# Causal self attention of a decoder layer: float32r halves kept in SBUF, heads paired in the array, query halves as the unit of order

## What is computed

```python
x = x + _L0_attn_ref(_layernorm(x, axis=-1), L0_attn_Wqkv, L0_attn_bqkv, L0_attn_Wout, L0_attn_bout)
# N_HEADS = 16, HEAD_DIM = 16
qkv = jnp.einsum('bsd,hde->bhse', x, Wqkv) + bqkv[None, :, None, :]
q, k, v = jnp.split(qkv, 3, axis=-1)
score = jnp.einsum('bhsd,bhtd->bhst', q, k)
score = jnp.where(causal[None, None], score, -jnp.inf)
attn = jax.nn.softmax(score / jnp.sqrt(jnp.asarray(HEAD_DIM, x.dtype)), axis=-1)
y = jnp.einsum('bhst,bhtd->bhsd', attn, v)
out = jnp.transpose(y, (0, 2, 1, 3)).reshape(b, s, d) @ Wout + bout
```

## Time and profile before

| what | us |
|---|---|
| median of 3 runs (1902.81 to 1908.55) | 1905.12 |
| the profiled execution's own time | 1912.87 |
| span of the profiled execution | 1911.2 |
| first score matmul starts, in the profile | 111.85 |
| first exponential starts | 156.14 |
| output projection's first transfer | 455.73 |

### The profile page before, as it was taken

One profiled execution on the slowest core, in us unless ns is written; L12 is line 12 of the kernel. 1 busy time (PEld: TensorE's weight loads), 2 busy tenths in 40 slices (PEclk: granted clock), 3 DMA queues, 4 the chain that ended last, 5 costly groups with the idle time before them and its releaser, 6 DMA issues. The chain is left out here.

```text
span 1911.2 us, 28538 instructions
## 1 busy us (share of the span) xinstructions
PE 1438.0 (75%) x10307; PEld 1073.4 (56%) x10307; DVE 1089.6 (57%) x2450; ACT 898.0 (47%) x2137; POOL 308.2 (16%) x338
## 2 busy tenths in 40 slices
PE   4758889988589999789981453588868059999964
PEld 2413333334379999656760231477755059999953
DVE  3657766741655555455668647456553047777753
ACT  1503555553256666331104775366542057887731
POOL 1200000002223333200001525100010600000034
PEclk8858999998799999979995665799887579999987
DMA  2371322200200000110000000211112256766623
GB/s 68 132 99 20 49 35 35 35 2 9 81 1 2 1 1 2 34 39 1 0 23 9 1 6 14 64 35 34 34 47 88 88 188 219 222 216 217 227 85 103
DMA packets 92688, 122.59 MB, mean 64 GB/s; under 512 B 22221, under 2 KB 74051, under 8 KB 92291
## 3 DMA queue, kind: packets, MB, share of 16 engines
q1 hardware_dynamic: 86675, 105.85, 20.5%
q0 software_dynamic: 4912, 14.42, 2.1%
q10 hardware_dynamic: 960, 0.47, 0.1%
HBM read 88.60 MB, written 24.67 MB: 59 GB/s over the span
## 5 line engine op out<-in xcount | busy, mean ns | idle before, releaser
L759 DVE TENSOR_REDUCE sa_top<-ps 128x1 f32<-128x512 f32 (+3 forms) x384 | 197.2, 553 | 96.3 <-PE ps L751 65.3
L787 ACT ACTIVATE sa_probs<-ps 128x1024 f32<-128x1024 f32 (+4 forms) x192 | 150.8, 811 | 204.1 <-PE ps L772 145.6
L751 PE MATMUL ps<-sa_k,sa_q 96*128 96x512 bf16 (+3 forms) x384 | 125.5, 365 | 55.5 <-DMA sa_k<-scr_k 28.5
L1983 PE MATMUL ps<-me_h,me_w_parts 128*128 128x256 f32 x1104 | 142.0, 289 | 14.5 <-DVE me_w_parts L2058 7.9
L1983 PEld LDWEIGHTS ps<-me_h,me_w_parts 128*128 128x128 f32 x1104 | 136.8, 192 | 18.7 <-issue 15.3
L1997 PE MATMUL ps<-me_w_parts,me_mid 128*128 128x256 f32 x1104 | 136.2, 283 | 6.1 <-DVE me_result L2075 6.1
L1997 PEld LDWEIGHTS ps<-me_w_parts,me_mid 128*128 128x128 f32 x1104 | 132.3, 188 | 10.5 <-issue 10.5
L2735 ACT ACTIVATE cx_p<-ps,cx_top 128x154 f32<-128x154 f32 x256 | 97.2, 389 | 86.4 <-DVE cx_top L2799 86.4
L751 PEld LDWEIGHTS ps<-sa_k,sa_q 96*128 96x128 bf16 x384 | 35.1, 98 | 160.7 <-DVE sa_top L759 89.1
L2058 DVE TENSOR_TENSOR me_w_parts<-me_chunk,me_w_parts 128x1024 fp32r<-128x1024 f32 x92 | 112.8, 1226 | 21.4 <-ACT me_w_parts L2023 18.6
L2045 ACT ACTIVATE me_full<-ps,me_b 128x256 f32<-128x256 f32 x184 | 95.0, 517 | 57.6 <-PE ps L1983 54.5
(11 more groups left out here) (397 smaller groups left out, 3530.7 us busy)
## 6 DMA issues: line engine op xcount, KB each, us to landing
me_chunk<-in_L_ffn_W_dram SPq DMA_DIRECT2D x92, 512.0 KB, 5.4
sa_q<-scr_q SPq DMA_DIRECT2D x48, 128.0 KB, 4.8
sa_k<-scr_k SPq DMA_DIRECT2D x48, 128.0 KB, 7.7
moe_rows<-mp_zeros SPq DMA_DIRECT2D x2, 2944.0 KB, 12.7
me_row<-moe_rows SPq DMA_DIRECT2D x23, 256.0 KB, 3.8
moe_results<-me_result POOLq DMA_DIRECT2D x23, 256.0 KB, 3.2
cn_qd<-cn_qh SPq DMA_DIRECT2D x64, 64.0 KB, 2.0
scr_q<-h_part SPq DMA_DIRECT2D x6, 512.0 KB, 3.9
```

The source lines that it names most:

```text
L751: last = pe.matmul(c.ps[:, bank, 0:w], self.q_st[0:96, slot, h, P * sb:P * sb + P], self.k_st[0:96, slot, h, k0:k0 + w], start=True, stop= ...
L759: return dve.tensor_reduce(self.top2[:, k0 // 512, ST * h + sb:ST * h + sb + 1], self.c.ps[:, bank, 0:w], AX.X, ALU.max)
L787: return act.activation(dst, src, ACT.Exp, scale=self.width ** -0.5)
L1983: last = pe.matmul(ps[:, MID + n % 4, 0:RT], w[:, u % 2, 0, i, DM * k + P * b:DM * k + P * b + P], h[:, u % 2, j, k, :], start=(m == 0), s ...
```

## The change

All of setup, context and projection becomes one stage, `front`, and `Attention` with its subclass becomes one class.

- `front` works by quarters of the tokens. x comes in four transfers, each with its own semaphore; the normalisation moves from DVE to ACT; normalised x and the weights are split into a high and a low half in float32r (ACT writes the high half, DVE the difference; POOL both for the weights). Each product is three float32r matmuls (high high, low high, high low) instead of one float32 matmul. Q and K come out as high (ACT) and low half (DVE) and stay in SBUF (`qk_high`, `qk_low`). The bias goes through DRAM once and comes back by five transfers. V gets 17 columns a head instead of 32.
- Staging copies from SBUF to SBUF: three stacks of 16 rows (high, low, high against high, high, low) for each of four heads of a unit, Q by SP, K by POOL, twelve transfers of 64 KB on each. The heads a = 0 and a = 1 of a pair lie at partitions 0 to 47 and 64 to 111, so a score matmul has 48 rows (50 with the two rows of the maximum), and each piece or chunk is now two matmuls, one for each head of the pair, into two banks.
- The grain is half a unit: 512 queries, 16 of them (`SUBS`). The pieces of one half run ahead of its chunks by one half. Exponentials have three buffers, a unit's half and key block each. The banks of pieces, turns and turns back form one ring of three. The count of reductions, masks, exponentials and weigh matmuls, and their widths, summed over a unit, stay as they are.
- The order of PE, DVE and ACT comes from `order()`, which lays out planned times for DVE and ACT with fixed costs and sorts.

The core of the diff:

```diff
+                for j, (i, m) in enumerate(blocks):
+                        terms = [(k, a, b) for k in range(KD) for a, b in ((wh, xh), (wh, xl), (wl, xh))]
+                        for n, (k, a, b) in enumerate(terms):
+                            last = pe.matmul(ps[:, bank, :], a[:, i, k, P * m:P * m + P], b[:, k, 512 * g:512 * g + 512],
+                                             start=(n == 0), stop=(n == len(terms) - 1))
...
+    def order(self):
+        items, dve, act = [], 0.0, 0.0
+        for k in range(len(SUBS)):
+            for n, (p, sb, k0, w) in enumerate(self.pieces(k)):
+                items.append((dve, "piece", k, n))
+                dve += 2 * (0.075 + w / 960)
+            items.append((dve, "join", k, 0))
+            items.append((dve + 1.2, "turn", k, 0))
+            dve += 1.0
+            act = max(act, dve + 5.0)
+            for n, (kb, p) in enumerate(self.chunks(k)):
+                items.append((act - 0.9, "chunk", k, n))
+                act += 0.12 + 2 * self.span(k, kb)[1] / 1200
+                if p == 1:
+                    items.append((act + 0.9, "weigh", k, kb))
+            items.append((act + 1.0, "copy", k, 0))
+            items.append((act + 3.0, "out", k, 0))
...
+                for a in range(2):
+                    pool.memset(self.k[64 * a + 32:64 * a + 64, :, :, :].bitcast(F32), 1.0).then_inc(s["made"].sem, 1)
+                pool.wait_ge(s["made"].sem, s["made"].at(2))
...
+                def take(m):
+                    if m >= self.MAX_RING:
+                        pe.wait_ge(s["freed"].sem, s["freed"].at(m - self.MAX_RING + 1))
+                    return m % self.MAX_RING
...
+                    banks = [take(m) for m in uses["piece", k, n]]
+                    for a in range(2):
+                        r = slice(64 * a, 64 * a + 3 * DH)
+                        last = pe.matmul(ps[:, banks[a], 0:w], self.q[r, slot, half, p, q0:q0 + P], self.k[r, slot, p, k0:k0 + w],
+                                         start=True, stop=not diagonal)
+                    if diagonal:
+                        for a in range(2):
+                            pe.matmul(ps[:, banks[a], w - P:w], c.identb[:, :], c.maxmask[:, :], start=False,
+                                      stop=True).then_inc(s["filled"].sem, 1)
...
-                last = pe.matmul(out[:, 0:qw], self.k_st[0:KROWS, slot, h, P * kb:P * kb + P],
-                                 self.q_st[0:KROWS, slot, h, P * kb + q0:P * kb + q0 + qw],
-                                 start=True, stop=q0 > 0)
```

More of the change, by code:

```diff
@@ L108, in new_stage @@
         self.signals = {}
[L111 to L152, removed]
 class LayerNorm:
@@ L230, in done, with front @@
             self.s[k].passed(n)
[L233 to L242, removed]
+VC = DH + 1
+def front(c, ct, hi, lo, v_all, scratch):
     nc, ps = c.nc, c.ps
     wqkv, bqkv = c.arg["L0_attn_Wqkv"], c.arg["L0_attn_bqkv"]
+    scr_b = scratch("scr_b0", [3, H, DH], F32)
+    G = NT // 4
@@ L246, in project_self @@
     with ExitStack() as ctx:
[L247 to L260, removed]
+        sb = lambda n, shape, dt=F32: c.sb(ctx, "fr_" + n, shape, dt)
+        raw_ctx = sb("ctx", [MH, 4, DC])
+        w = sb("w", [P, KD, H, 3 * DH])
+        wh, wl = sb("wh", [P, 3, KD, D], F32R), sb("wl", [P, 3, KD, D], F32R)
+        bias, bias_v = sb("b", [P, 2, KD]), sb("bv", [P, H, DH])
+        stats, mv = sb("stats", [P, NT, 6]), sb("mv", [P, NT, 2])
@@ L266, in _ @@
+                sp.dma_start(raw_ctx[:, :, :], c.arg["ctx_768"].rearrange("b (i m) d -> m (b i) d", m=MH)).then_inc(c_in.sem, 16)
+                sp.wait_ge(b_out.sem, b_out.at(16))
                 for i in range(2):
[L267 to L278, removed]
+                    for m in range(KD):
+                        sp.dma_start(bias[:, i, m:m + 1],
+                                     scr_b[i, 8 * m:8 * m + 8, :].rearrange("h (e a) -> (h e) a", a=1)).then_inc(b_in.sem, 16)
@@ L292, in _ @@
             @block.tensor
             def _(pe):
[L294 to L309, removed]
@@ L815, in _ @@
+                pe.wait_ge(const.sem, const.at(2))
+                turn(0)
                 pe.wait_ge(c_in.sem, c_in.at(16))
@@ new lines, in self_layer @@
+def self_layer(c, ct, scratch):
+    with ExitStack() as c0:
+        o_tok = c.sb(c0, "o_tok0", [P, NT, D], F32)
+        with ExitStack() as c1:
+            v_all = c.sb(c1, "v_all0", [P, NT, H, VC], F32)
+            hi, lo = c.sb(c1, "qk_high", [P, 2 * KD, N], F32R), c.sb(c1, "qk_low", [P, 2 * KD, N], F32R)
+            front(c, ct, hi, lo, v_all, scratch)
+            c.new_stage()
+            SelfAttention(c, c1, v_all, hi, lo, o_tok).run()
+        c.new_stage()
+        project_out(c, "po0", o_tok, KD, c.arg["L0_attn_Wout"], c.arg["L0_attn_bout"])
```

839 lines of the change are left out of this document (408 added, 431 removed).

## The result

| | us |
|---|---|
| before, median of 4 runs | 1904.49 |
| after, median of 4 runs (1951.86 to 1983.10) | 1971.08 |
| ratio after to before, 95% interval | 1.031 (1.024 to 1.039) |
| the profiled execution after: own time, span | 1968.88, 1966.8 |
| predicted | 1833 (1788 to 1880) |

A forecast was written before the change was run, and what follows sets the result against it. No engine is full; the loop from exponential to weigh step sets attention's pace. First score 83 + half speed 4 + eight units 276 + tail 20 = 383 us instead of 455.2; 1905 - 72 = 1833 us, range 1788 to 1880.

The forecast's parts named there:

- Front: Start to end of projection: first projection matmul at 16 us, end at 59 us instead of 84.1.
- Staging: Between front and attention: POOL's fill 10.5 us, twelve copies 8.6, landing 4; first score at 83 us instead of 111.85.
- Prices at full clock: PE's costs in attention: pair 0.25 us, shape change 0.1 us; a unit 32.4 us.
- the 0.1 us I took: PE in attention: cost of each of 64 shape changes a unit around masks, 6.4 us a unit.
- my 0.25 us: PE in attention: a pair of matmuls side by side; 48 pairs, 12 us a unit.
- my sum for PE: PE's work a unit in attention: pairs 12, masks 3.8, weighing 8.8, turns 1.4, shape changes 6.4: 32.4 us.
- The rate of 34.5 us a unit: Attention: PE's 32.4 us plus 2 us of ring waits a unit; 276 us for eight units.
- the opposite as a rival: Attention: PE does not get the 2.4 GHz level, 58 us a unit, 2021 us in all; chance 0.05.
- a clock below 1.0: Sign that the prediction is wrong: granted clock under 1.0 in the steady part of attention.
- the ring: Attention: small waits of PE for three banks, of which a pair takes two; 2 us a unit.
- Tail: After the last reduction, to the output projection: 20 us instead of 39.7.
- Buffers of exponentials: Attention: with three buffers, ACT's wait for the weigh step, 7.3 us a unit, goes.

The follow-up runs named there:

- full_spread: Changed kernel with every piece and chunk matmul over 128 rows, not side by side (other numbers as scores), and the later order: 1900.99 us.
- before_48: Kernel before, with pieces and chunks over 48 of their 96 and 99 rows: 2086.72 us.
- experiment 13: Changed kernel in its own order; PE asks for a pair's second bank only when it comes to the second matmul: 1915.02 us.
- 8 to 10: Experiments on the changed kernel: full_spread (1900.99 us); the later order with banks taken one at a time (1918.16 us); full_split (1863.04 us).
- the later order: Changed kernel's planned order with chunks of every fourth half spaced 3.3 times as wide, the others 1.12 times; alone against the changed kernel: 1939.53 us.
- full_split: full_spread with each piece's bank taken one at a time and each mask right behind its own matmul: 1863.04 us.
- zero_slots: zero_rows with three slots for Q and K's slot released when its last chunk is scored: 1882.50 us, ratio to before 0.991.
- zero_rows: Changed kernel, pairs not side by side: zeros at the other head's rows, two slots, the later order, banks taken one at a time: 1975.12 us.

## Why the prediction was wrong, step by step

- **Front: right, 5 us short.** First projection matmul at 18.2 us (16 predicted), end at 64.5 us (59).
- **Staging: right.** The fill took 10.48 us (10.5). POOL issues its twelve copies in 6.0 us (8.6), the first score follows 5.4 us behind them (4) and stands at 86.7 us (83). First exponential 106.4 us (98).
- **Prices at full clock: near, 2 us a unit short.** PE's timeline of after, three stretches in which nothing is waited for:

```profile
205.29 0.49 PE L614 MATMUL ps<-sa_q,sa_k 50*128 50x512 f32 x2
205.72 0.28 PE L618 MATMUL ps<-expmask,identb 128*128 128x128 bf16 x2
205.94 0.41 PE L629 MATMUL ps<-sa_probs,v_all 128*17 128x128 f32 x8
206.28 0.50 PE L587 MATMUL ps<-sa_k,sa_q 48*128 48x512 f32 x2
206.62 0.33 PE L614 MATMUL ps<-sa_q,sa_k 50*128 50x384 f32 x2
...
209.59 0.44 PE L587 MATMUL ps<-sa_k,sa_q 48*128 48x384 f32 x2
209.97 0.28 PE L593 MATMUL ps<-maxmask,identb 128*128 128x128 bf16 x2
210.18 1.05 PE L629 MATMUL ps<-sa_probs,v_all 128*17 128x512 f32 x8
211.16 0.38 PE L614 MATMUL ps<-sa_q,sa_k 50*128 50x256 f32 x2
211.48 0.28 PE L618 MATMUL ps<-expmask,identb 128*128 128x128 bf16 x2
211.70 0.33 PE L614 MATMUL ps<-sa_q,sa_k 50*128 50x128 f32 x2
211.96 0.28 PE L618 MATMUL ps<-expmask,identb 128*128 128x128 bf16 x2
...
300.08 0.80 PE L587 MATMUL ps<-sa_k,sa_q 48*128 48x512 f32 x2
300.80 1.05 PE L629 MATMUL ps<-sa_probs,v_all 128*17 128x256 f32 x8
301.79 0.79 PE L614 MATMUL ps<-sa_q,sa_k 50*128 50x512 f32 x2
302.51 0.40 PE L618 MATMUL ps<-expmask,identb 128*128 128x128 bf16 x2
```

  A wide pair costs 0.34 us where another pair follows (206.28 to 206.62) and 0.43 us where a mask follows (205.29 to 205.72), so a change of shape is near the 0.1 us I took. The pair is above my 0.25 us, and above the 0.22 us that I had estimated by the Trainium skill (TensorE: Matmul & The Clock Gate, Part 3: Packing small matmuls), with a start distance of 0.21 us put in for the duration of a matmul. With a mask behind them, pairs of 384, 256 and 128 columns cost 0.38, 0.32 and 0.26 us, a pair of masks 0.21 us, a weigh step of 512 columns 0.98 us. By these prices a unit is an estimated 34 us (32 pairs with a mask 11.1, 16 wide pairs 5.4, masks 6.9, weighing 9.2, turns 1.5), where my sum for PE was 32.4: some 16 us in eight units that I had put too low. In the lower rows, at a clock of 0.50, a wide pair costs 0.72 us, both to a weigh step and to a mask. One after the other, over 128 rows, such a pair cost 0.54 to 0.64 us at full clock (`full_spread`, 310.31 to 310.85 and 313.69 to 314.33 us).
- **The step that failed: the clock.** The rate of 34.5 us a unit took the 2.4 GHz level for granted. I had the opposite as a rival, with 58 us a unit and a chance of 0.05, and dismissed it by "233 of 259 us busy went with 0.99, and a PE at half speed would be full, which is when the clock rose". The first half read the earlier trace rows of a stream of 96 and 99 rows as if it spoke for one of 48. The second is refuted outright: 10.00 busy of 10 at 0.50 here, 143.45 of 144 at 0.58 in `before_48`. I had named a clock below 1.0 as a sign that the prediction is wrong, and it is the sign that came. The trace of before had no matmul of fewer than 96 rows in this stage, so it could not bear a chance as low as 0.05. The Trainium skill (TensorE: Matmul & The Clock Gate, Part 1: The HAM clock gate) has the clock follow how busy PE has recently been; with PE busy all of 144 us and a clock of 0.58, `before_48` doesn't agree with that.
- **How much that is.** A mean of 0.68 over 98 to 440 us is 36% of the time at 1.00 and 64%, 219 us, at 0.50. If PE had set the pace all through, full clock would have halved those: an estimate of 110 us in this window. It is an upper one, since at full clock the stretches of pieces are bounded by DVE (1.29 us for a wide pair).
- **The second miss: the ring.** I put 2 us a unit, 16 in all, on "small waits of PE for the ring of three banks". PE's matmuls stood idle for DVE for 42.3 us, which holds up the chunks behind them, so ACT waits as well. The single edit of experiment 13 brings that to 1.2 us and gives 56 us back, some of it by the higher clock. At the upper level the edit, with the masks moved too, is worth 38 us (8 to 10). The 110 us and the 56 us overlap and can't be added.
- **Tail.** Last reduction 491.7, projection 519.2: 27 us, where 20 were predicted.
- **Buffers of exponentials: right.** ACT no longer waits for the weigh step, which it did for 7.3 us a unit.

With both causes out, and the later order, `full_split` has the projection at 418.9 us and 1863 us in all: 108 of the 138 us. For the last 30 I hold that its matmuls are not side by side (0.54 to 0.64 us a wide pair instead of 0.34 to 0.43); that pairs at full clock would give them back is argued from these prices, not shown, since no run kept the upper level with them.

## What to carry to other kernels

Two small matmuls side by side took 0.34 to 0.43 us instead of 0.54 to 0.64 us at full clock, but with them the clock stood at 0.50 for most of the stage: before a stream is cut to half the array's rows, run the old kernel with its operands cut to those rows and read the granted clock. A clock level read from one kernel's rows may speak only for instructions of that form. And where work goes in pairs through a ring with an odd number of buffers, ask for each buffer at the instruction that writes it; asking for two ahead stalls an in-order engine with all that stands behind.

## What the runs showed of the hardware

- Over 156 to 415 us of one program, pieces and chunks over 48 rows had a granted clock of 0.61 with PE 99% busy (0.55 and 98% with the masks over 48 rows too), over 65 rows 0.95 with PE 90% busy, over 96 and 99 rows 0.99 with PE 90% busy.
- Matmuls over 96 and 100 rows, half of them multiplied with zeros, had 0.92 over 98 to 440 us (`zero_slots`).
- Pairs over 48 and 50 rows at two halves of the array reach the level of 1.00 in stretches, and stayed at 0.50 from 270 to 340 us with PE busy 9.1 to 10 of each 10 us.
- The copies that stage K, 64 KB each from SBUF to SBUF, cost POOL 0.48 us each to issue, not the 0.71 us of its DRAM transfers in the earlier trace rows.
- A fill of 96 rows of 4096 elements in POOL takes 3.5 us, one of 32 rows of 6144 elements 5.2 us: its time goes by the elements of a row, 0.85 ns each, and not by the number of rows (6.96 us for two in `zero_rows`, 10.48 us for two in after).
